# A GNN chain on one core: 105 of a partition's 392 edge records ordered by one-hot matmuls in place of scatters

## What is computed

```python
h_fwd = h @ W_forward.T
h_rev = h @ W_reverse.T
messages = h_fwd[src] * direction[:, 0:1] + h_rev[src] * direction[:, 1:2]
scores = leaky_relu(einsum('ef,hf->eh', messages, attn_forward[0]), 0.2)
exp_scores = exp(scores - scores.max(axis=0))
sum_exp = segment_sum(exp_scores, dst, N)
norm = exp_scores / (sum_exp[dst] + 1e-10)
outs = [segment_sum(messages * norm[:, hd:hd+1], dst, N) for hd in range(H)]
```

## Time and profile before

| | us |
|---|---|
| median of three runs | 4309.44 (4303.3 to 4314.62) |
| the profiled execution, its own time | 4311.09 |
| its span, first to last instruction | 4309.3 |
| busy: PE / DVE / ACT / POOL | 2747.5 / 3230.9 / 2438.4 / 1489.8 |
| POOL: indirect adds, L429, 392 | 622.7 |
| POOL: gathers of rows, L942, 416 | 461.8 |
| POOL: record scatters, L130, 392 | 387.0 |

### The profile page before, as it was taken

How to read it: one execution, slowest core, us unless ns; L and a number is a source line. 1 busy time by engine, 2 the same in 40 slices (tenths; PEclk the granted TensorE clock), 3 DMA queues, 4 the chain that set the end, 5 groups by cost and what they waited for, 6 DMA issues and landing times. The chain is left out here.

```text
span 4309.3 us, 74123 instructions
## 1 busy us (share of the span) xinstructions
PE 2747.5 (64%) x27274; PEld 2432.7 (56%) x27274; DVE 3230.9 (75%) x5570; ACT 2438.4 (57%) x4647; POOL 1489.8 (35%) x1221
## 2 busy tenths in 40 slices
PE   1223222018860156655569999699986999769997
PEld 1112111014440133433469998699986999769997
DVE  4999666125230277777599996999969999879998
ACT  1223212020020245444289996799967999769997
POOL 2777888867667777776000000000000000000000
PEclk9999999999985576676689998899988999879999
DMA  7223222217710122222102211021120211202122
GB/s 291 35 26 52 34 34 9 0 2 192 185 23 9 42 50 49 50 50 40 36 15 75 60 55 58 13 77 53 55 64 14 77 53 55 66 11 68 55 60 63
DMA packets 330243, 243.48 MB, mean 57 GB/s; under 512 B 86728, under 2 KB 318410, under 8 KB 328906
## 3 DMA queue, kind: packets, MB, share of 16 engines
q1 hardware_dynamic: 243060, 185.47, 14.7%
q0 software_dynamic: 82304, 29.95, 7.2%
q10 hardware_dynamic: 4566, 23.91, 1.4%
HBM read 211.56 MB, written 27.68 MB: 56 GB/s over the span
## 5 line engine op out<-in xcount | busy, mean ns | idle before, releaser
L429 POOL DMA_INDIRECT table<-adj_value,adj_cell x392 | 622.7, 1589 | 219.1 <-issue 217.6
L942 POOL DMA_INDIRECT l_row<-node_rows,l_rec x416 | 461.8, 1110 | 132.9 <-issue 126.2
L485 PE MATMUL adj_ps<-adj_pair,adj_same 128*128 128x2 bf16 x2940 | 132.4, 165 | 574.0 <-DVE adj_same L660 509.3
L660 DVE TENSOR_SCALAR_CACHE_REDUCE adj_same<-adj_rows,adj_key 128x1792 bf16<-128x1792 f32 (+1 forms) x392 | 448.7, 1209 | 60.1 <-DMA adj_rows<-key_rows 49.4
L956 PE MATMUL l_ps<-l_value,l_hot 128*128 128x260 f32 x832 | 344.6, 576 | 182.4 <-issue 95.2
L1483 PE MATMUL g3a_ps<-g_parts,g3a_pos 128*128 128x195 bf16 x2500 | 429.6, 248 | 38.1 <-DVE g3a_side L1589 36.9
L1483 PE MATMUL g1a_ps<-g_parts,g1a_pos 128*128 128x195 bf16 x2500 | 429.0, 248 | 34.6 <-DVE g1a_side L1589 33.1
L1483 PE MATMUL g2a_ps<-g_parts,g2a_pos 128*128 128x195 bf16 x2500 | 427.8, 248 | 35.9 <-DVE g2a_side L1589 34.3
L1483 PE MATMUL g0a_ps<-g_parts,g0a_pos 128*128 128x195 bf16 x2500 | 427.8, 248 | 35.9 <-DVE g0a_side L1589 34.4
L485 PEld LDWEIGHTS adj_ps<-adj_pair,adj_same 128*128 128x128 bf16 x2940 | 110.9, 104 | 596.2 <-issue 592.2
L130 POOL DMA_INDIRECT records<-rec,place x392 | 387.0, 987 | 160.9 <-issue 111.4
(11 more groups left out here) (389 smaller groups left out, 6753.7 us busy)
## 6 DMA issues: line engine op xcount, KB each, us to landing
gcn_cols<-table SPq DMA_DIRECT2D x24, 1600.0 KB, 8.3
g_cols<-table SPq DMA_DIRECT2D x32, 1024.0 KB, 5.5
adj_rows<-key_rows SPq DMA_DIRECT2D x28, 896.0 KB, 4.4
table<-zeros ACTq DMA_DIRECT2D x8, 2512.5 KB, 27.1
g_cols<-table SPq DMA_DIRECT2D x16, 1152.0 KB, 5.9
g_cols<-table SPq DMA_DIRECT2D x24, 768.0 KB, 4.8
g_er<-er_rows SPq DMA_DIRECT2D x64, 256.0 KB, 3.5
g_cols<-table SPq DMA_DIRECT2D x12, 864.0 KB, 5.1
```

Of the source, the lines that this page charges most:

```text
L429: pool.indirect_dma_start(out=table.rearrange("(w o) -> w o", o=1), out_offset=bass.IndirectOffsetOnAxis(cell[:, u, k:k + 1], 0), in_=valu ...
L485: last = pe.matmul(ps[:, u, 2 * k:2 * k + 2], same[:, r * GT + k, :], equal, start=(j == 0 and k == 0), stop=False, skip_group_check=True)
L660: dve.tensor_scalar(same[:, r * GT + j:(r + 1) * GT, :].rearrange("p k q -> p (k q)"), rows[:, u, j * P:GT * P], key[:, bass.ds(n * GT + j ...
L942: pool.indirect_dma_start(out=row[:, u, k, :], out_offset=None, in_=node_rows, in_offset=bass.IndirectOffsetOnAxis(rec[:, j, 0:1].bitcast( ...
```

## The change

The last 105 of a partition's 392 columns (`SORTED` = 5 columns for each of 21 chunks) are no longer scattered; `scatter_records` stops at `SCATTERED` = 287. Their records are put in order by matmuls, in the last 20 groups of `adjacency` and once behind them. For each of the 5 columns of a chunk DVE makes two one-hot matrices by comparison, the slot within a tile (`spot_hot`, 128 wide) and the tile (`tile_hot`, 416 wide), in 16-bit types. ACT makes 9 scaled copies of `spot_hot` (`weigh`), scaled by the 9 values that a record is split into: source in two parts, destination, and each attribute in three parts. PE sums `weighted` times `tile_hot` into four PSUM banks (`ps_s`), 45 matmuls of 416 columns in bfloat16 for a chunk, four behind each count step. DVE makes the operands of chunk n-6 behind the cells of group n, ACT scales them there, and PE sums them in group n+1, at whose start it waits for them. At the end DVE copies the four sums out, SP writes them to DRAM (`records_by_matmul`), and `edge_layer` reads both arrays and adds them.

To make room in PSUM, the four slots of `ps` share two banks, and `ps_t` and `ps_r` lie in the banks of `ps_s`; PE then waits for the copy of the counts two groups back. 18 small operations in `rank` prepare the values.

```diff
+SORT = 5
+SORTED = SORT * (G - 8 + 1)
+SCATTERED = T - SORTED
+VALUES = 9
+PLANE = [0, 0, 1, 2, 2, 2, 3, 3, 3]
...
-    for t in range(records.next, min(records.next + n, T)):
+    for t in range(records.next, min(records.next + n, SCATTERED)):
...
+        ps_c = s.ps("ps_c", [P, 2, 512])
+        ps = [ps_c[:, u % 2, u // 2 * 64:u // 2 * 64 + 2 * GT] for u in range(SLOTS)]
+        ps_s = s.ps("ps_s", [P, 4, 512])
...
+            sync.wait_ge(ordered_ready, 1)
+            sync.dma_start(records.by_matmul, ordered).then_inc(ordered_out, 16)
+            sync.wait_ge(ordered_out, 16)
...
+            def sort_some(u, lo, hi):
+                for a in range(lo, min(hi, SORT * VALUES)):
+                    k, c = divmod(a, VALUES)
+                    last = pe.matmul(ps_s[:, PLANE[c], 0:TILES], weighted[u % 2][:, k, c, :], tile_hot[u % 2][:, k, :], start=False, stop=True,
+                                     skip_group_check=True)
+                    if a == SORT * VALUES - 1:
+                        last.then_inc(sort_used, 1)
+            def sort_operands(m):
+                pe.wait_ge(weighted_ready, m)
...
+                pe.wait_ge(tile_ready, m)
...
-                    pe.wait_ge(values_ready, n + 1)
+                    pe.wait_ge(values_ready, n + 1 + 2)
                     pe.sem_inc(pe_pass, 1)
+                    if sorting:
+                        sort_operands(i * SLOTS + (u - 7))
...
+                            last.then_inc(same_used, 1)
+                            if sorting:
+                                sort_some(u, 4 * j, 4 * j + 4)
...
             with pe.Fori(2, CELL_TURNS) as i:
-                turn(i)
+                turn(i, sorting=True)
+            sort_operands(G - 8 + 1)
+            sort_some(0, 0, SORT * VALUES)
...
+            def weigh(v, m, t):
+                act.wait_ge(spot_ready, m)
...
+                act.wait_ge(sort_used, m)
...
+                for k in range(SORT):
+                    for c in range(VALUES):
+                        last = act.activation(weighted[v][:, k, c, :], spot_hot[v][:, k, :], ACT.Copy, scale=values[:, c, bass.ds(t + k, 1)])
+                last.then_inc(weighted_ready, 1)
...
+                    act.copy(value[:, u, :], ps[u][:, 0:2 * GT:2]).then_inc(values_ready, 1)
+                    if sorting:
+                        weigh((u + 1) % 2, i * SLOTS + (u - 6), i * (SLOTS * SORT) + (u - 7) * SORT)
...
+            def hot_of(v, m, t):
+                dve.wait_ge(sort_used, m)
+                for k in range(SORT):
+                    last = dve.tensor_scalar(spot_hot[v][:, k, :], number16[:], spot[:, bass.ds(t + k, 1)], None, ALU.is_equal)
+                last.then_inc(spot_ready, 1)
+                for k in range(SORT):
+                    last = dve.tensor_scalar(tile_hot[v][:, k, :], tile16[:], tile_f[:, bass.ds(t + k, 1)], None, ALU.is_equal)
+                last.then_inc(tile_ready, 1)
...
                     cells(n, u)
+                    if sorting:
+                        hot_of((u + 1) % 2, i * SLOTS + (u - 6), i * (SLOTS * SORT) + (u - 7) * SORT)
...
+            dve.tensor_copy(ordered.rearrange("p (c j) -> p c j", c=4), ps_s[:, :, 0:TILES]).then_inc(ordered_ready, 1)
...
         def _(sync):
-            sync.wait_ge(records.scattered, T * 16)
+            sync.dma_start(value[:].rearrange("p v k f -> p (v k f)")[:, 0:4 * TILES], records.by_matmul).then_inc(rec_in, 16)
+            sync.wait_ge(records.scattered, SCATTERED * 16)
             sync.dma_start(rec[:], records.dram.rearrange("(p j) c -> p j c", p=P)).then_inc(rec_in, 16)
...
-            pool.wait_ge(rec_in, 16)
+            pool.wait_ge(rec_ready, 1)
...
-            act.wait_ge(rec_in, 16)
+            act.wait_ge(rec_ready, 4)
...
+            dve.wait_ge(rec_in, 32)
+            dve.tensor_tensor(rec[:, :, 0].bitcast(I32), rec[:, :, 0].bitcast(I32), more[:, 0, :], ALU.add).then_inc(rec_ready, 1)
+            dve.tensor_tensor(rec[:, :, 1], rec[:, :, 1], more[:, 1, :], ALU.add).then_inc(rec_ready, 1)
+            for c in range(2):
+                dve.tensor_tensor(rec[:, :, 2 + c], rec[:, :, 2 + c], more[:, 2 + c, :], ALU.add).then_inc(rec_ready, 1)
```

More of the change, by code:

```diff
@@ L307, in _, with adjacency @@
             dve.wait_ge(taken, NB)
-def adjacency(nc, src, dst, attr, table, table_zero, zeros, room, key_rows, ident, dinv, records, nodes, nodes_loaded):
+def adjacency(nc, src, dst, attr, table, table_zero, zeros, room, room2, key_rows, ident, dinv, records, nodes, nodes_loaded):
     with ExitStack() as ctx:
@@ L342, in adjacency @@
         one = s.sb("one", [P, 1], F32)
-        nothing = s.sb("nothing", [P, P], BF16)
+        nothing = s.sb("nothing", [P, TILES], BF16)
         away = s.sb("away", [P, 2, GT, P], BF16)
@@ L457, in _ @@
             pe.sem_inc(hot_used, 2)
-            pe.wait_ge(numbers_set, 4)
-            pe.matmul(ps_deg[:, 0:NB], nothing[:], nothing[:, 0:NB], start=True, stop=False, skip_group_check=True)
+            pe.wait_ge(numbers_set, 6)
+            pe.matmul(ps_deg[:, 0:NB], nothing[:, 0:P], nothing[:, 0:NB], start=True, stop=False, skip_group_check=True)
             def rank_sums():
@@ L493, in turn @@
                             k = half * RING + r
-                            last = pe.matmul(ps[:, u, 2 * k:2 * k + 2], own[:, half, r, :], earlier, start=False,
+                            last = pe.matmul(ps[u][:, 2 * k:2 * k + 2], own[:, half, r, :], earlier, start=False,
                                              stop=(half == 1), skip_group_check=True)
@@ L508, in _ @@
             rank_sums()
+            pe.wait_ge(ranked, 1)
+            pe.sem_inc(sort_used, 2)
+            for plane in range(4):
+                pe.matmul(ps_s[:, plane, 0:TILES], nothing[:, 0:P], nothing[:], start=True, stop=True, skip_group_check=True)
             with pe.Fori(2, CELL_TURNS) as i:
-                turn(i)
+                turn(i, sorting=True)
+            sort_operands(G - 8 + 1)
+            sort_some(0, 0, SORT * VALUES)
         @block.scalar
@@ L540, in _ @@
                     act.sem_inc(act_pass, 1)
-                    act.copy(value[:, u, :], ps[:, u, 0:2 * GT:2]).then_inc(values_ready, 1)
+                    act.copy(value[:, u, :], ps[u][:, 0:2 * GT:2]).then_inc(values_ready, 1)
+                    if sorting:
+                        weigh((u + 1) % 2, i * SLOTS + (u - 6), i * (SLOTS * SORT) + (u - 7) * SORT)
+            with act.Fori(0, 2) as i:
+                turn(i)
+            weigh(0, 1, 0)
+            with act.Fori(2, CELL_TURNS) as i:
+                turn(i, sorting=True)
             act.wait_ge(hot_used, 2 + G)
@@ L571, in _ @@
             dve.wait_ge(places_set, 3)
[L572 removed]
+            dve.wait_ge(numbers_set, 6)
             dve.tensor_scalar(node_b[:], node_b[:], 1.0 / P, None, ALU.mult).then_inc(places_set, 1)
@@ L587, in cells @@
                 dve.wait_ge(cells_free, n + 1)
-                dve.scalar_tensor_tensor(pick[:, u, :], onward[:, u, :], -1.0, ps[:, u, 1:2 * GT:2], ALU.add, ALU.is_gt).then_inc(picked, 1)
+                dve.scalar_tensor_tensor(pick[:, u, :], onward[:, u, :], -1.0, ps[u][:, 1:2 * GT:2], ALU.add, ALU.is_gt).then_inc(picked, 1)
                 dve.wait_ge(picked, n * 2 + 1)
@@ L904, in edge_layer @@
         value = s.sb("value", [P, 2, LG, MW], F32)
+        more = value[:].rearrange("p v k f -> p (v k f)")[:, 0:4 * TILES].rearrange("p (c j) -> p c j", c=4)
         number_i = s.sb("number_i", [P, P], I32)
@@ L1644, in program @@
                 nodes_loaded = nc.alloc_semaphore("nodes_loaded")
-                adjacency(nc, a["src"], a["dst"], a["edge_attr_2"], cells, table_zero, zeros, h, key_rows, ident, dinv, records,
+                adjacency(nc, a["src"], a["dst"], a["edge_attr_2"], cells, table_zero, zeros, h, f1, key_rows, ident, dinv, records,
                           (x, a["x"], w1, a["L0_gnn_W1"]), nodes_loaded)
```

71 lines of the change are left out of this document (53 added, 18 removed).

## The result

| | before | after |
|---|---|---|
| median of the runs shown, us | 4308.66 (4303.3 to 4314.62) | 4184.14 (4181.12 to 4189.74) |
| ratio, 95% interval | 1 | 0.9708 (0.9694 to 0.9721) |
| profiled execution, its span, us | 4311.1, 4309.3 | 4189.7, 4187.9 |

The change makes the kernel 2.9% faster: 124.5 us by the medians, 121.4 us between the two profiled executions. On a second chip the same two kernels stood at 4185.15 and 4317.36, ratio 0.9695 (0.9683 to 0.9708).

The account below looks back on a forecast made before the run. POOL was taken to bound `adjacency`, with 104 scatters standing alone at the start of `edge_layer`. 4309.4 - 131 for those + 5 for DVE slowing POOL = 4183 us; 8-in-10 range 4168 to 4225.

Parts of the forecast that it names:

- the head of `edge_layer`: Start of `edge_layer`: 104 scatters leave the path, first gather at 1306.1 instead of 1437.3 us, gaining 131 us.
- the chain: `adjacency`: loop through DVE, ACT and PE from one `counted` to the next, 28.7 us against POOL's 28.9, costing nothing.
- DVE against POOL: `adjacency`: the new compares slow POOL's indirect adds, 0 to 16 us in 20 groups, taken as 5 us.
- Rival 4: Start of `edge_layer`: not shortened, two reads or another wait take the scatters' place; 4309 us; chance 0.03.
- The condition: `adjacency`: the DVE, ACT and PE loop must keep under 29.3 us; beyond, each 0.1 us costs 1.9 us.
- rival 1: `adjacency`: the DVE, ACT and PE loop exceeds POOL's group, at 31.1 us 4217, at 34.9 us 4289; chance 0.19.
- The worse half of rival 1: `adjacency`: PE's bursts stay at 1.2 GHz throughout, loop 34.9 us, cost 106 us, time 4289; chance 0.04.
- the sign: `adjacency`: in the profile after, DVE's wait before pick is for POOL and not for PE.
- ACT's copies: `adjacency`: 45 scaled copies of 128 columns a group at 0.300 us each, 13.5 us.
- rival 2: `adjacency`: ACT's scaled copies cost 0.507 us each like L188, loop 38.0 us, 4343 us, slower than before; chance 0.05.
- Rival 3: `adjacency`: DVE's compares hold POOL back in full, +16 us (4194), or 50 us by the shared-port rule (4228); chance 0.13.
- Start and end: `adjacency`: rank ends at 292.8 us, group 8 ready at 321.4, group 27 at 866.7, last write 898, before POOL's 906.8.

Follow-up runs that it names:

- experiment 2: Changed kernel with all 392 records scattered again and the sorted sums multiplied by zero: 4316.96 us, ratio 1.0005 to the kernel before.
- experiment 1: Kernel before without its last 105 scatters and without sorting, those records missing from the output: 4182.24 us, ratio 0.9698.
- six-record run: Changed kernel with six records a group sorted by matmuls in place of five, sums still among the counts: 4266.87 us, ratio 0.9889.
- four-record run: Changed kernel with four records a group sorted by matmuls in place of five: 4209.33 us, ratio 0.9757.
- late sums: Changed kernel, a group's 45 sums moved behind its edge and degree counts: 4181.66 us; there with DVE's compares made once 4186.47, twice a group 4183.37.

## Why the prediction came out right

The time, 4184.14 us against 4183, and the range hold, and so does the main mechanism: the scatters at the head of `edge_layer` go, and the chain stays just under POOL's group. That the two times agree within 1.2 us is luck. The executions of one kernel spread over 8 to 11 us, and what was added for DVE against POOL was 5 us where 1 was measured. By the prediction's own steps:

- **The head of `edge_layer`.** 131 us predicted, 131.1 measured; experiment 2, with the scatters back, shows that it is they, and experiment 1 that little else is in it. Inside, small errors cancel: the reads landed a little sooner than assumed (without the memset DVE begins 6.8 us behind the first issue, not 7.2), DVE's memset was overlooked (0.35 us), and the first add was taken at 0.6 us to its end and took 0.87. Rival 4 is out.
- **The chain.** 28.7 us predicted, 28.99 measured. PE's part, 13.1 predicted with 4 us of slow pace, is 13.1 in the mean, though no burst is: they take 12.7 and 13.7 us in turn. What was short is the rest, from the pick to PE's first matmul, at 15.6 (0.7 + 1.0 + 13.5 + 0.4) against 15.9: in the link shown DVE took 1.9 for 1.7, ACT 13.2 for 13.5, and the handovers the remainder. The condition, under 29.3, held by 0.3 us; group 27 was ready at 873.2 and not at 866.7. That the condition is real was shown by the six-record run: a chain of 33.3 gives (33.3 - 29.3) x 19 = 76 us by the prediction's rule, measured 79.8. So rival 1 was one record away. The Trainium skill, page "TensorE: Matmul & The Clock Gate", section "What's actually happening", has the throttled state as the default; the start of every burst agrees, four sums in 1.55 us before four in 0.86. The worse half of rival 1, slow throughout, is out.
- **One reading of it was wrong.** The prediction said that DVE's wait before pick would be for POOL and not for PE. Of its 20 waits there, 3.18 us each, the trace puts 15 down to PE, 5 to issue and none to POOL. DVE meets POOL there only once it is some three groups, 87 us, ahead. A chain 0.2 us a group faster than POOL, as predicted, gains 4 us in the 20 groups, and one that is 0.04 faster, as measured, not even 1. So the sign contradicted the prediction's own 28.7 and 28.9, while the time did not depend on it. The same error is in the expectation of the four-record run.
- **ACT's copies.** 0.300 predicted, 13.24/45 = 0.294 measured, as the Abs of the same width and not as L188: rival 2 is out.
- **DVE against POOL.** 5 us predicted; the stage ended 1.4 us late and the block of `edge_layer` began 1.0 late, while the mean add grew from 1563 to 1577 ns. The term was too large by some 4 us, and its mechanism is not borne out: on the late sums 4.6 us more of these compares in a group did not lengthen the mean add (1562 and 1559 ns), so the rate of 0.32, which came from scans, does not hold for them. What lengthens the changed kernel's adds stays open. The Trainium skill, page "SBUF — State Buffer", section "🔬 SBUF: two separate sides", has a DVE operation in a two-port mode shut GpSimd out for its whole length. Of the loss that the prediction worked out from it nothing shows: doubling the compares, 2.3 us a group, cost 0.1. An add beside five of them, 1.27 us together, took 1.70 us in place of 1.55; the 0.15 us are less than the length of one compare (0.25), so no trace here tells whether a single one holds an add back. Rival 3 is out in both forms, 16 us and 50.
- **Start and end.** The rank ended at 292.7 (292.8 predicted). Group 8 was to be ready at 321.4 (the terms given add up to 321.2); its pick began at 321.69. The last copy and write (DVE until 899.6, then SP) were over before POOL's last scatter, as the sum had it.

## What to carry to other kernels

At the head of `edge_layer` POOL issued scatters while the other engines stood idle. Taking 131 us out of that stretch was worth some 520 us more of ACT and PE in a stage where both had time to spare. Before adding work to engines with slack, draw the loop from one release to the next through all of them: the sum along the loop must stay under the period of the engine that bounds the stage. Work moved behind the release leaves the loop, which made even six records a group nearly free. And stop where the removed work was hidden: a sixth record a group gained nothing.

## What the runs showed of the hardware

One stretch of the changed kernel by windows (busy us and count of PE, PEld, DVE, ACT, POOL; then the granted clock); the row of before is in the earlier trace rows. Below it, PE's first burst of sums, by windows and as a line of the timeline:

```profile
355.00:908.00 553.00, 252.64 (x3249) 157.40 (x3249) 375.95 (x794) 359.36 (x1137) 458.74 (x306) 0.69 0.26 26
```

```profile
307.90:311.00 3.10, 3.03 (x34) 1.76 (x35) 1.78 (x3) 3.10 (x12) 2.49 (x3) 1.00 0.19 5
```

```profile
308.34 1.55 PE L508 MATMUL adj_ps_s<-h 128*128 128x416 bf16 x4
```

The granted clock reads 0.69 where before it read 1.00, though before the one wide matmul of `adjacency`, at 251 us, ran at the slower pace. The changed kernel's first burst shows the same within itself: four sums in 1.55 us, the slow pace, under a granted clock of 1.00. A reading of 1.00 was no evidence of 2.4 GHz ahead of the first fall that the trace shows; a matmul's duration was. After that fall the two agree, 0.50 beside 1.55 us and 1.00 beside 0.86. The slow start of a burst was longer than the 2.9 us that the attention layer showed: 6.4 and 4.3 us in the two bursts shown, behind 15.40 and 15.42 us of idling.
